# A graph network's attention stage: when VectorE makes the messages, and when ScalarE copies the exponentials

## The reference, cut to what matters

```
ke    = k[src] + edge_attr * We
alpha = (q[dst] . ke) / sqrt(d)                # a number for each edge and head
m     = segment_max(alpha, dst)
ex    = exp(alpha - m[dst])
w     = ex / segment_sum(ex, dst)[dst]
agg   = segment_sum(w * (v[src] + edge_attr * We), dst)
out   = layernorm((agg + skip) @ Wo + bo + x)
```

## Time and profile before

| | |
|---|---|
| time, median of three runs | 6159.68 us |
| profiled execution, its span | 6159.3 us |
| busy, share of the span | TensorE 63%, VectorE 59%, ScalarE 46%, GpSimd 71% |
| attention stage | about 163 to 1420 us |
| VectorE's adds in it (L1215) | 0.30 us each, 880 |
| VectorE's messages (L1198) | 0.68 us each, 220 |
| ScalarE's copies of exponentials (L1019) | 0.24 us each, 220 |

### The profile page before, as it was taken

How to read it: one execution, slowest core, us unless ns; L and a number is a source line. 1 busy time by engine, 2 the same in 40 slices (tenths; PEclk the granted TensorE clock), 3 DMA queues, 4 the chain that set the end, 5 groups by cost and what they waited for, 6 DMA issues and landing times. The chain is left out here.

```text
span 6159.3 us, 93437 instructions
## 1 busy us (share of the span) xinstructions
PE 3901.9 (63%) x20652; PEld 3181.0 (52%) x20652; DVE 3661.3 (59%) x11663; ACT 2833.9 (46%) x6936; POOL 4388.1 (71%) x4477
## 2 busy tenths in 40 slices
PE   5567766765666666768878877334444346766665
PEld 4566666654555555545655555233333346665443
DVE  6788888886888888767777675111101124445665
ACT  3788888881111111255555554111111148784443
POOL 3676777654777777757777776677777777777775
PEclk8787887787888888878898887555555569898877
DMA  4444444454645555542222224322222235553223
GB/s 125 124 132 126 129 128 127 127 103 125 171 133 136 139 136 134 145 66 73 74 74 74 74 74 66 96 77 76 76 75 75 74 108 167 163 165 88 58 58 46
DMA packets 485366, 649.31 MB, mean 105 GB/s; under 512 B 120187, under 2 KB 332938, under 8 KB 484822
## 3 DMA queue, kind: packets, MB, share of 16 engines
q0 software_dynamic: 155552, 345.75, 22.1%
q1 hardware_dynamic: 329271, 297.58, 17.7%
HBM read 495.44 MB, written 150.71 MB: 105 GB/s over the span
## 5 line engine op out<-in xcount | busy, mean ns | idle before, releaser
L692 POOL DMA_INDIRECT e_ring<-table,gather_i x880 | 921.5, 1047 | 287.3 <-issue 267.5
L692 POOL DMA_INDIRECT kv_ring<-keys_values,gather_i x880 | 864.1, 982 | 365.2 <-issue 248.0
L2099 POOL DMA_INDIRECT rows_by_src<-arena,key x880 | 870.9, 990 | 310.2 <-issue 260.3
L692 POOL DMA_INDIRECT e_ring<-filter_rows,gather_i x880 | 840.7, 955 | 304.5 <-issue 268.1
L692 POOL DMA_INDIRECT arena<-table,gather_i x880 | 858.7, 976 | 278.9 <-issue 265.9
L2083 PE MATMUL rs_ph<-nodes,arena 128*128 x1664 | 424.4, 436 | 668.1 <-ACT arena L2092 615.2
L2083 PEld LDWEIGHTS rs_ph<-nodes,arena 128*128 128x128 f32 x1664 | 365.7, 324 | 727.4 <-issue 727.2
L2075 DVE TENSOR_SCALAR arena<-arena,part 128x512 f32<-128x512 bf16 x220 | 113.2, 518 | 949.0 <-PE rs_ph L2083 898.8
L1562 PE MATMUL e_pa<-e_msg,e_hot 128*128 128x128 f32 x3520 | 559.9, 311 | 35.8 <-DVE e_msg L1764 28.2
L741 DVE TENSOR_TENSOR arena<-arena,e_pa 128x128 f32 x1760 | 495.0, 281 | 114.0 <-PE e_pa L1562 68.9
L2325 PE MATMUL gl_sum_f<-arena,gl_hot_f 128*128 128x128 f32 x1760 | 283.0, 311 | 425.0 <-DMA arena<-table,gather_i 191.0
(11 more groups left out here) (461 smaller groups left out, 9863.7 us busy)
## 6 DMA issues: line engine op xcount, KB each, us to landing
rows_by_src<-e_filler SPq DMA_DIRECT2D x256, 260.0 KB
arena<-rows_by_src SPq DMA_DIRECT2D x256, 260.0 KB
at_rows<-local_rows SPq DMA_DIRECT2D x220, 128.0 KB, 3.5
e_rows<-local_rows SPq DMA_DIRECT2D x220, 128.0 KB
arena<-local_rows SPq DMA_DIRECT2D x220, 128.0 KB, 3.3
e_attr<-edge_attr SPq DMA_DIRECT2D x880, 25.0 KB
kv_ring<-keys_values,gather_i POOLq DMA_INDIRECT x880
e_ring<-table,gather_i POOLq DMA_INDIRECT x880
```

What stands on the lines that cost most here:

```text
L692: pool.indirect_dma_start(ring[:, r, u, :], None, table, bass.IndirectOffsetOnAxis(index, 0)).then_inc(arrived[r], 16)
L2099: pool.indirect_dma_start(self.table, bass.IndirectOffsetOnAxis(place, 0), self.out[:, r, u, :], None, bounds_check=SLOTS_R - 1, oob_is_er ...
```

## The change

On ScalarE, `exps` of batch s - 8 moves from behind turned_hot(s + 1) and keep_values(s - 1) to right behind edge_hot(s - 8). On VectorE, `weigh` and `message` of batch s - 8 move from between and behind the adds to the front of the slot: in slots 1, 2 and 3 ahead of products(s - 1) (behind the scans, where there are any), in slot 0 right behind products(s - 1). The adds 2 and 3 then follow each other, in slot 0 adds 1, 2 and 3.

```diff
                 if 0 <= s - LAG < BATCHES:
                     edge_hot(s - LAG)
+                    exps(s - LAG)
                 if s + 1 < BATCHES:
                     turned_hot(s + 1)
                 if 0 <= s - 1 < BATCHES:
                     keep_values(s - 1)
-                if 0 <= s - LAG < BATCHES:
-                    exps(s - LAG)
...
                 if chain and ph == 3:
                     scan_all(n)
+                weighing = 0 <= km < BATCHES
+                if weighing and ph != 0:
+                    weigh(km)
+                    message(km)
                 if 0 <= s - 1 < BATCHES:
                     products(s - 1)
+                if weighing and ph == 0:
+                    weigh(km)
+                    message(km)
                 if adding and ka % CB == 0:
                     rescale(ka // CB, which[0])
...
                 if chain and ph == 3:
                     shift(n)
-                if 0 <= km < BATCHES:
-                    weigh(km)
                 if adding:
                     add(ka, 2, which[2])
-                if 0 <= km < BATCHES:
-                    message(km)
-                if adding:
                     add(ka, 3, which[3])
```

## The result

The changed kernel takes 6199.47 us, the median of five runs (6183.84 to 6208.28); the ratio to the kernel before is 1.0061, 95% interval 1.0049 to 1.0073. A second set of runs beside a fresh set of before gave 1.0049 (1.0036 to 1.0061). So it is slower by 0.5 to 0.6%, some 30 to 38 us (40 between the medians of five runs each, 6159.68 before); the forecast was 6193. The profiled execution has a span of 6190.2 us for 6159.3, 30.9 more. Lines of stage_attention's VectorE part stand one lower than before: L1214 is the add, L1197 the message, L1192 weigh, L1128 products.

What follows compares the result with a forecast made beforehand. The attention stage was taken as a VectorE chain with TensorE pushing in at five places. The sum was 6159.3 - 75 + 65 + 44 = 6193 us, range 6130 to 6240, the forecast's own 6175 to 6218.

Steps and rivals of the forecast that it cites:

- The gain: VectorE's waits for TensorE at five lines of the attention stage, 99.4 us in all, fall by 26 + 49 = 75 us.
- the other four: VectorE's waits for TensorE at L1161, L1215, L1149 and L1206, 54.4 us in all: 5 remain, so 49 gained.
- The working for slot 3: TensorE's total starts right behind the carries, 0.6 us earlier; VectorE reaches L1180 0.5 later; 1.1 less for each of 26 waits.
- Cost 1: VectorE's adds stand one behind another, each waiting for the one before: 1.18 us a chunk, x 55 = 65 us.
- The distances of the drain: Spacing of bare adds taken from the drain: second add 0.46 us after the first, 0.51 between adds of different pairs.
- Cost 2: Register loads at VectorE's slot starts lose their cover behind add 3: 44 us, between 0 and 59.
- Rival 1: VectorE's queue absorbs the loads: cost 2 is 0, cost 1 about 40 or whole; 6124 to 6149 us; chance 0.21.
- Rival 2: The terms cancel within 12 us: costs of 70 to 90 by a gap of 0.4 between adds; 6160 us; chance 0.17.
- Rival 3: TensorE isn't freed, total's second half waits for the last add: five waits fall by half only, 50; 6218 us; chance 0.12.
- the five waits: VectorE's waits for TensorE at L1180, L1161, L1215, L1149 and L1206, 99.4 us in all before the change.
- Rival 4: TensorE stays at its lower clock level behind a longer gap ahead of the carries: 6193 + 55 = 6248 us; chance 0.07.

Runs made afterwards that it cites:

- run with both changes: Changed kernel with the four adds each put behind a long instruction and register reads moved early, against the kernel before: 0.9857, 6084.16 us.
- adds-apart run: Changed kernel with the four adds each put behind a long instruction, register reads left at the slot's start, against the kernel before: 0.9962, 6149.64 us.

## Why the prediction was right

**The account.** The forecast moved the time by -75 + 65 + 44 = +34 us. The trace has the waits for TensorE at -68.0 (102.5 to 34.5), and +26.8 at the last add. So the costs together are 26.8 + 68.0 = 95 us, for 109; with the small waits for ScalarE and for keys they are 97, which is also what VectorE's own steps grew by (1107.6 to 1204.3). The mechanism of each term is what the runs show. The sum came out near because gain and costs were both put too high, by 7 and by 12; that the errors cancel in part is luck.

**The gain.** 75 forecast, 68 measured. L1180's line was put at 19 (45 less 26) and has 15.6; the other four were to keep 5 and keep 15 (L1160 7.8, L1148 5.7, the adds 1.5; 4 more stand at other lines), since L1160 and L1148 still have single long waits of up to 2.1 us. The working for slot 3 held: total starts right behind the carries.

**Cost 1.** The distances of the drain hold in the whole stage: 0.46 and 0.51. With them the sum per chunk is that of the forecast but for 0.44 instead of 0.46 behind the walk. All of VectorE's steps but those in which the reads lie grew by 55 us: the steps of adds, weigh and message by 59, and some 5 came off the step behind products, which the forecast didn't have. The run with both changes gives 62, the adds-apart run about 69.

**Cost 2.** The steps in which the reads lie grew by 42 us, for 44; the issue gaps, which leave out all below 0.15 us, by 35.4. The single prices were right: 0.49 for 0.22 behind a plain add 3 and 0.70 for 0.33 before first_norm. First_norm's steps grew by 18 us, as forecast. Plain slots had 17 for 21, since in 17 of them VectorE waited for TensorE at that place before, and the end of such a wait is booked as gain. Join behind renew_nodes had 8 for 5 (0.70 for 0.34), the next slot behind renew_nodes 3 for nothing; behind the other node work 4 came off.

**The rivals.** Rival 1 needed the instruction behind add 3 to start after 0.22; it starts after 0.49. Its 40 us for adds 0.39 apart was too low by its own working (0.07 less in 220 slots takes 15 from the 65); that changes nothing here. Rival 2 needed costs of 70 to 90 us; they were 97. The rule of the Trainium skill's Perfetto Trace Analysis (Per-engine timelines) that the sequencer decodes on while an instruction waits in its queue would have made the reads free, if each wait is held by the VectorE instruction itself. The runs show the reads to be bare behind an instruction that waits, 0.5 to 0.7 us to the next start, and covered when they stand ahead of it; for this stage the measurement decides. In the program each wait is a call of its own (`wait_ge`), and no run tells whether it is this wait or the read that holds up what follows. Rival 3 was half right in its mechanism: total is held by the adds at both halves, 86.4 us of TensorE's time; but the five waits didn't stop at half of their 99.4 us, they fell to 30.6. Rival 4's mechanism is there as well: TensorE's wait ahead of the carries grew from 86.9 to 131.5 us, and the median matmul of total takes 309 ns for 288 (the kernel before, then the changed one):

```profile
L928 PE MATMUL at_pa<-at_msg,at_hot x1760: 284/288/611, 203.5 to 1414.3; 128*128 128x145 f32 x196
L928 PE MATMUL at_pa<-at_msg,at_hot x1760: 284/309/611, 200.9 to 1441.4; 128*128 128x145 f32 x196
```

The granted clock over 500 to 800 us is 0.75 (0.79 before), and 0.82 over the next 300 (0.83 before). The Trainium skill's rule that gaps between bursts bring the clock down (TensorE: Matmul & The Clock Gate, Why this matters for your kernels) goes the same way. VectorE's waits for TensorE fell all the same; what the lower clock took from the gain no run shows.

## What to carry to other kernels

Ahead of moving a long instruction, ask what short things it covers where it stands: here a message of 0.6 us hid both an add's wait for the add before it and four register reads, and freeing 68 us of waits cost some 97 us of uncovered ones. Read registers for the next step behind a long instruction, ahead of the first instruction that has to wait; that alone turned a 0.6% loss into a 1.3% gain. Two fixes on one engine don't add up when a third engine's pace is near: here the gains end at about 1.4%, with GpSimd's gathers at their own pace.

## What the runs showed that I had not expected

Early reads were worth 97 us at the last add in the new order and 33 in the old: as long as VectorE runs into TensorE's waits, more than half of what it saves is given back there (25 of 46 us), and once TensorE is ahead almost nothing is (10 of 92). And the early reads still leave adds 2 and 3 0.46 apart. Putting them apart then saved VectorE 62 us of its own steps and the kernel next to nothing, because with early reads alone GpSimd's gathers set the pace already.
